# VectorE's operations with two SBUF operands given PSUM operands, and the five mixed streams finished by VectorE

## The reference

```python
# layer 0, per batch
x = x + attention(layernorm(x) -> q, k, v; 16 heads of 16, one mask for all batches) @ w_ao + b_ao
x = x + attention(layernorm(x) -> q; encoder -> k, v; mask per batch) @ w_co + b_co
#   scores = q.k / 4 * mask - 10000 * (1 - mask), softmax over the keys
x = x + gelu(layernorm(x) @ w1 + b1) @ w2 + b2
# layer 1, per batch (32 heads of 8)
xn = layernorm(x); sx = shift(xn) - xn
m  = tanh((xn + sx * maa_x) @ maa_w1) @ maa_w2            # five streams
x5 = xn + sx * (maa_stack + m)                            # w, k, v, r, g
w  = exp(-exp(td + tanh(x5[1] @ decay_w1) @ decay_w2))
r, k, v, g = x5[3] @ Wr.T, x5[0] @ Wk.T, x5[2] @ Wv.T, silu(x5[4] @ Wg.T)
# over the tokens: out = r.(u * k v + s); s = k v + w * s
x = x + (groupnorm over 8(out) * gn_w + gn_b) * g @ Wo.T
xn = layernorm(x); sx = shift(xn) - xn                    # then a gated squared-relu layer
x = x + sigmoid((xn + sx * fmr) @ Wr2.T) * (square(relu((xn + sx * fmk) @ Wk2.T)) @ Wv2.T)
```

## Time and profile before

| | |
|---|---|
| time, median of 3 runs | 743.11 us (741.23 to 743.57) |
| the profiled execution's own time | 742.92 us |
| its span, first to last instruction | 741.1 us |
| PE busy | 646.6 us (87% of the span) |
| DVE busy | 592.4 us (80%) |
| ACT busy | 574.4 us (78%) |
| POOL busy | 368.8 us (50%) |
| mean granted TensorE clock | 0.945 of full speed |

### The profile page before, as it was taken

How to read it: one execution, slowest core, us unless ns; L and a number is a source line. 1 busy time by engine, 2 the same in 40 slices (tenths; PEclk the granted TensorE clock), 3 DMA queues, 4 the chain that set the end, 5 groups by cost and what they waited for, 6 DMA issues and landing times. The chain is left out here.

```text
span 741.1 us, 16759 instructions
## 1 busy us (share of the span) xinstructions
PE 646.6 (87%) x5585; PEld 542.6 (73%) x5585; DVE 592.4 (80%) x1434; ACT 574.4 (78%) x2002; POOL 368.8 (50%) x537
## 2 busy tenths in 40 slices
...
GB/s 302 319 34 8 2 69 62 62 68 52 86 18 120 2 136 2 136 1 138 1 124 13 94 44 79 59 65 74 31 106 2 136 1 128 2 128 5 123 8 7
DMA packets 54844, 52.76 MB, mean 71 GB/s; under 512 B 6127, under 2 KB 49511, under 8 KB 54375
## 3 DMA queue, kind: packets, MB, share of 16 engines
...
## 5 line engine op out<-in xcount | busy, mean ns | idle before, releaser
L1067 ACT ACTIVATE SC<-SC,NMX 128x128 f32<-128x128 f32 x512 | 198.8, 394 | 6.8 <-DVE NMX L822 6.5
L1067 ACT ACTIVATION_READ_ACCUMULATOR SC<-SC,NMX 128x1 f32 x512 | 99.1, 194 | 0.0
L557 PE MATMUL PS_T<-CST,SC 128*128 128x128 f32 x512 | 81.3, 283 | 15.8 <-ACT SC L1067 6.4
L822 DVE TENSOR_REDUCE NMX<-SC 128x4 f32<-128x512 f32 x128 | 85.0, 668 | 3.4 <-POOL SC L1239 3.1
L799 DVE TENSOR_TENSOR SC<-PS_S,MASK 128x512 f32<-128x512 f32 x128 | 82.8, 670 | 5.9 <-PE PS_S L539 5.9
L1075 ACT ACTIVATE PT<-PS_T 128x512 f32<-128x512 f32 x128 | 77.0, 601 | 11.2 <-PE PS_T L557 10.2
L557 PEld LDWEIGHTS PS_T<-CST,SC 128*128 128x128 f32 x512 | 59.2, 144 | 30.6 <-ACT SC L1067 16.2
L894 DVE TENSOR_TENSOR_SCAN SS<-W,AJ 128x1024 f32<-128x1024 f32 x32 | 73.2, 2286 | 2.5 <-DVE AJ L887 0.5
L469 PE MATMUL PS_B<-B_LT,W 128*128 128x128 f32 x512 | 67.7, 290 | 7.5 <-ACT B_LT L1023 7.4
L469 PEld LDWEIGHTS PS_B<-B_LT,W 128*128 128x128 f32 x512 | 63.6, 203 | 11.4 <-ACT B_LT L1023 11.0
L1289 POOL TENSOR_TENSOR SS<-SS,KR 128x1024 f32<-128x1024 f32 x16 | 37.8, 2364 | 55.9 <-DVE SS L894 55.9
...
## 6 DMA issues: line engine op xcount, KB each, us to landing
...
```

The costliest lines, as they stand in the source:

```text
L557: last = pe.transpose(PS_T[:, j * T:(j + 1) * T], SC[:, nr(b, a) % 2, g, j, :], ident)
L822: dve.tensor_reduce(NMX[:, nr(b, a) % 2, GH * g:GH * g + GH], SC[:, nr(b, a) % 2, g], AX_X, ALU.max, negate=True)\
L1067: last = act.activation(SC[:, nr(b, a) % 2, g, j, :], SC[:, nr(b, a) % 2, g, j, :], ACT.Exp, bias=NMX[:, nr(b, a) % 2, h:h + 1], accum_out ...
```

## The change

- The three masks of `DVE_ADDS` are multiplied in place in PSUM, and their add reads PSUM and writes `SC`. The wait for the free half of `SC` moves from the multiplication to the add. TensorE's next writers of those banks wait for the add (`scores_read`).
- `b_streams` works in place in PSUM. `b_addnorm` goes to VectorE: three operations (128 x 512, 128 x 512, 128 x 256) from PSUM and `XN` into `MX`. The fifth stream's `b_low2`, `b_decay1` and `b_keyrec` wait for the first, second and third of them.
- `d_ruk` becomes one operation without u, which goes into a selector `USEL` made once; VectorE's `d_own` becomes one operation instead of two; `d_norm` goes from GpSimd to VectorE.
- The small tiles `GM`, `GV` and `GY` of the group norm move from SBUF to the last columns of `PS_D`; ScalarE's `d_affine` writes `PS_D` instead of SBUF, and `d_gated` reads it there.
- Five small steps of GpSimd (the mask's 10000*(mask-1), the copies of the previous rows, of the first columns and of the first states) go to ScalarE; the one-time scaling of `fv` moves into `d_shift`.
- All five order lists are new. They begin at another point of the round, so lags in them aren't those of the lists before.

```diff
 SP_ORDER = [
+    ("d_store", 0, 6), ("b_wspread", 0, 3), ("a_load", 0, 0), ("b_vstore", 0, 3), ("b_vspread", 0, 3)]
 PE_ORDER = [
+    ("b_low2", 0, 4), ("a_prob_turn", (1, 1), 3), ("d_own", 0, 5), ("a_scores", 0, 1), ("a_prob_turn", (1, 2), 3),
+    ("b_low2", 2, 4), ("d_read", 0, 5), ("a_prob_turn", (1, 3), 3), ("b_decay1", 0, 4), ("d_oturn", 0, 5),
+    ("b_decay2", 0, 4), ("a_pv", 1, 3), ("a_enc_turn", 0, 2), ("b_keyrec", 0, 4), ("b_keyrec", 1, 4),
+    ("a_out", 1, 3), ("a_turn", 1, 2), ("b_valgate", 0, 4), ("b_valgate", 1, 4), ("a_val", 1, 2), ("a_key", 1, 2),
+    ("a_prob_turn", (0, 0), 1), ("a_query", 1, 2), ("d_yturn", 0, 5), ("a_prob_turn", (0, 1), 1), ("a_scores", 1, 2),
+    ("d_out", 0, 5), ("b_turn", 0, 3), ("a_prob_turn", (0, 2), 1), ("b_mlp1", 0, 3), ("a_turn", 0, 0),
+    ("b_mlp1", 1, 3), ("b_mlp2", 0, 3), ("d_turn", 0, 5), ("a_prob_turn", (0, 3), 1), ("b_mlp2", 1, 3),
+    ("a_query", 0, 0), ("a_pv", 0, 1), ("d_keyrec", 0, 5), ("b_turn", 1, 3), ("a_val", 0, 0), ("d_keyrec", 1, 5),
+    ("a_key", 0, 0), ("a_out", 0, 1), ("b_low1", 0, 3), ("d_val", 0, 5), ("a_prob_turn", (1, 0), 2)]
 DVE_ORDER = [
+    ("a_normal", 0, 1), ("d_sum", 0, 6), ("a_mask", (1, 1), 3), ("a_mask", (1, 2), 3), ("a_maxima", (1, 0), 3),
+    ("d_stats", 0, 6), ("a_mask", (1, 3), 3), ("d_moments", 0, 6), ("a_addmask", (1, 3), 3), ("d_ruk", 0, 5),
+    ("a_inverse", 0, 2), ("a_maxima", (1, 1), 3), ("d_normal", 0, 6), ("d_outer", 0, 5), ("d_scan", 0, 5),
+    ("b_sum", 0, 4), ("b_stats", 1, 4), ("d_mixed", 0, 6), ("b_moments", 1, 4), ("a_query", 0, 1),
+    ("a_maxima", (1, 2), 3), ("b_normal", 1, 4), ("d_mixed", 1, 6), ("d_outer", 1, 5), ("a_maxima", (1, 3), 3),
+    ("a_context", 0, 2), ("b_mixed", 0, 4), ("d_rstate", 0, 5), ("a_sum", 0, 2), ("d_scan", 1, 5),
+    ("d_mixing", 0, 6), ("a_stats", 1, 2), ("b_streams", 0, 4), ("a_moments", 1, 2), ("b_addnorm", 0, 4),
+    ("d_own", 0, 5), ("b_streams", 1, 4), ("b_addnorm", 1, 4), ("b_streams", 2, 4), ("a_mask", (0, 0), 1),
+    ("a_inverse", 1, 3), ("a_mask", (0, 1), 1), ("d_output", 0, 5), ("a_addmask", (0, 1), 1), ("b_addnorm", 2, 4),
+    ("d_means", 0, 5), ("d_centre", 0, 5), ("a_maxima", (0, 0), 1), ("a_context", 1, 3), ("d_spread", 0, 5),
+    ("a_normal", 1, 2), ("a_maxima", (0, 1), 1), ("d_guess", 0, 5), ("d_guess", 1, 5), ("a_mask", (0, 2), 1),
+    ("a_mask", (0, 3), 1), ("d_guess", 2, 5), ("d_newton", (0, 0), 5), ("a_stats", 0, 0), ("d_newton", (0, 1), 5),
+    ("a_moments", 0, 0), ("d_newton", (0, 2), 5), ("a_sum", 1, 3), ("d_newton", (1, 0), 5), ("b_stats", 0, 3),
+    ("d_newton", (1, 1), 5), ("d_newton", (1, 2), 5), ("a_addmask", (0, 3), 1), ("d_newton", (2, 0), 5),
+    ("d_newton", (2, 1), 5), ("b_moments", 0, 3), ("d_newton", (2, 2), 5), ("d_norm", 0, 5), ("a_maxima", (0, 2), 1),
+    ("a_query", 1, 2), ("a_maxima", (0, 3), 1), ("d_gated", 0, 5), ("b_normal", 0, 3), ("b_gate", 0, 4),
+    ("a_mask", (1, 0), 2)]
 ACT_ORDER = [
+    ("b_scale", 0, 3), ("a_exps", (0, 3, 0), 1), ("a_exps", (0, 3, 1), 1), ("b_gelu", 0, 3),
+    ("a_prob_copy", (0, 2), 1), ("b_gelu", 1, 3), ("a_scale", 0, 0), ("d_scale", 0, 5), ("a_prob_copy", (0, 3), 1),
+    ("a_exps", (1, 0, 0), 2), ("a_widen", 0, 1), ("a_exps", (1, 0, 1), 2), ("a_exps", (1, 1, 0), 2),
+    ("a_spread", 0, 1), ("b_scale", 1, 3), ("a_exps", (1, 1, 1), 2), ("d_keyrec", 0, 5), ("a_val", 0, 0),
+    ("d_relu2", 0, 5), ("a_exps", (1, 2, 0), 2), ("a_exps", (1, 2, 1), 2), ("b_low", 0, 3), ("a_key", (0, 0), 0),
+    ("a_prob_copy", (1, 0), 2), ("a_key", (0, 1), 0), ("a_exps", (1, 3, 0), 2), ("a_prob_copy", (1, 1), 2),
+    ("d_own", 0, 4), ("a_exps", (1, 3, 1), 2), ("a_prob_copy", (1, 2), 2), ("d_ocopy", 0, 4),
+    ("d_first_states", 0, 3), ("b_decay1", 0, 3), ("a_prob_copy", (1, 3), 2), ("a_widen", 1, 2), ("b_decay2", 0, 3),
+    ("b_decays", 0, 3), ("a_lessmask", 0, 1), ("a_spread", 1, 2), ("d_squares", 0, 4), ("a_enc_copy", 0, 1),
+    ("a_exps", (0, 0, 0), 0), ("b_keyrec", 0, 3), ("a_exps", (0, 0, 1), 0), ("a_scale", 1, 1),
+    ("a_exps", (0, 1, 0), 0), ("b_values", 0, 3), ("a_exps", (0, 1, 1), 0), ("a_val", 1, 1), ("b_gatetanh", 0, 3),
+    ("a_key", (1, 0), 1), ("a_prob_copy", (0, 0), 0), ("a_key", (1, 1), 1), ("d_affine", 0, 4),
+    ("a_exps", (0, 2, 0), 0), ("a_exps", (0, 2, 1), 0), ("a_prob_copy", (0, 1), 0)]
 POOL_ORDER = [
+    ("a_addmask", (0, 2), 1), ("a_addbias", 0, 1), ("b_root", 0, 3), ("d_final", 0, 6), ("a_root", 0, 0),
+    ("b_addbias", 0, 3), ("a_addmask", (1, 0), 2), ("a_addmask", (1, 1), 2), ("a_addmask", (1, 2), 2),
+    ("d_root", 0, 5), ("d_shift", 0, 5), ("b_root", 1, 3), ("b_shift", 0, 3), ("d_rstate", 0, 4),
+    ("a_addmask", (0, 0), 0), ("a_root", 1, 1), ("a_addbias", 1, 2)]
...
+        USEL = sb("USEL", [CT, P // RS])
...
+        GM, GV, GY = (PS_D[:, 512 - n * RH:512 - (n - 1) * RH] for n in (1, 2, 3))
...
+        def scores_read(pe, n, g):
+            if n >= 0:
+                b, a = turn_of(n)
+                if (a, g) in DVE_ADDS:
+                    pe.wait_ge(a_dadded, nth(DVE_ADDS, b, (a, g)))
+                else:
+                    pe.wait_ge(a_masked, 4 * n + g + 1)
...
             def a_query(b, a):
-                pe.wait_ge(a_masked, 4 * nr(b, a))
+                scores_read(pe, nr(b, a) - 1, 3)
...
             def b_low2(b, n):
-                    pe.wait_ge(b_mix, 3 * b + 1)
+                    pe.wait_ge(b_mx, 3 * b + 1)
...
             def b_decay1(b, _):
-                pe.wait_ge(b_mx, 3 * b + 1)
-                pe.wait_ge(b_mix, 3 * b + 2)
+                pe.wait_ge(b_mx, 3 * b + 2)
...
-                    pe.wait_ge(b_mx, 3 * b + 2)
-                    pe.wait_ge(b_mix, 3 * b + 3)
+                    pe.wait_ge(b_mx, 3 * b + 3)
...
-                    last = pe.matmul(PS_D[:, t * (P // RS):(t + 1) * (P // RS)], RK[:, t, :], hsel,
+                    last = pe.matmul(PS_D[:, t * (P // RS):(t + 1) * (P // RS)], RK[:, t, :], USEL[:, t, :],
...
-                dve.tensor_tensor(SC[:, nr(b, a) % 2, g], PS_S[:, g], over_heads(mask), ALU.mult).then_inc(a_masked, 1)
+                masked = PS_S[:, g] if arg in DVE_ADDS else SC[:, nr(b, a) % 2, g]
+                dve.tensor_tensor(masked, PS_S[:, g], over_heads(mask), ALU.mult).then_inc(a_masked, 1)
...
-                dve.tensor_tensor(SC[:, nr(b, a) % 2, g], SC[:, nr(b, a) % 2, g], over_heads(MADD[:, b % 2 if a else 2, :]), ALU.add)\
+                if nr(b, a) > 1:
+                    dve.wait_ge(a_turned, 4 * nr(b, a) + g - 7)
+                dve.tensor_tensor(SC[:, nr(b, a) % 2, g], PS_S[:, g], over_heads(MADD[:, b % 2 if a else 2, :]), ALU.add)\
...
-                        last = dve.scalar_tensor_tensor(MX[:, i, t, :], PS_B[:, n % 2, at:at + T], col("stack", 2 * i + t),
-                                                        SX[:, t, :], ALU.add, ALU.mult)
+                        last = dve.scalar_tensor_tensor(PS_B[:, n % 2, at:at + T], PS_B[:, n % 2, at:at + T],
+                                                        col("stack", 2 * i + t), SX[:, t, :], ALU.add, ALU.mult)
...
+            def b_addnorm(b, n):
+                dve.wait_ge(b_mix, 3 * b + n + 1)
+                i, k = MIX_TURNS[n][0], len(MIX_TURNS[n])
+                dve.tensor_tensor(MX[:, i:i + 3 * k - 2:3], PS_B[:, n % 2, 0:k * C].rearrange("p (k t n) -> p k t n", t=CT, n=T),
+                                  XN[:, :, 1:T + 1].unsqueeze(1).to_broadcast([P, k, CT, T]), ALU.add).then_inc(b_mx, 1)
...
+                dve.tensor_tensor(RK[:, :, :], KR[:, 1], KR[:, 0], ALU.mult).then_inc(d_rk, 1)
...
+                dve.tensor_tensor(heads(CV[:, :]), heads(PS_D[:, C:2 * C]), over_tokens(OW[:, :], RH, RS), ALU.mult)\
+                    .then_inc(d_cv, 1)
...
+            def d_norm(b, _):
+                dve.wait_ge(d_gr, 12 * b + 12)
+                dve.tensor_tensor(heads(O[:, :]), heads(O[:, :]), over_tokens(GY[:, :], RH, RS), ALU.mult)\
+                    .then_inc(d_n, 1)
...
-                dve.scalar_tensor_tensor(YT[:, :, :], YA[:, :, :], 0.5, tiles(G[:, :]), ALU.mult, ALU.mult)\
+                dve.scalar_tensor_tensor(YT[:, :, :], tiles(PS_D[:, C:2 * C]), 0.5, tiles(G[:, :]), ALU.mult, ALU.mult)\
...
+                act.activation(PREV[:, b, :, :], tiles(values)[:, :, 0:2], ACT.Copy).then_inc(a_prev, 1)
...
+                act.activation(MADD[:, b % 2, :], MASK[:, b, :], ACT.Copy, bias=-10000.0, scale=10000.0)\
+                    .then_inc(a_less, 1)
...
+                    act.activation(XN[:, :, 0:1], PREV[:, b, :, 1:2], ACT.Copy)
...
+                act.activation(AJ[:, :, :, 0:1], S0[:, b, :, :].unsqueeze(3), ACT.Copy).then_inc(d_s0, 1)
...
+                    last = act.activation(PS_D[:, C + t * T:C + (t + 1) * T], PS_D[:, t * T:(t + 1) * T], ACT.Identity,
...
+                act.activation(XM[:, :, 0:1], PREV[:, b, :, 0:1], ACT.Copy)
```

(13 more changed lines are left out.)

135 lines of the change are left out of this document (32 added, 103 removed).

## The result

The changed kernel takes 735.15 us (median of 5 runs, 734.43 to 736.32), the kernel before 741.84 beside it on the same chip: ratio 0.9909, 95% interval 0.9886 to 0.9933. It is faster by 0.9%, 6.7 us. The profiled execution took 736.32 us, its span is 734.5; before, 742.92 and 741.1.

What follows compares the result with a forecast made beforehand. It saw three nearly full engines, with hand-overs between VectorE, GpSimd and TensorE setting the 39.24 us period. A period of 38.8 gave -5.3 us, the drain +0.4, so 742.92 became 738; own range 734 to 741, 80% range 729 to 751.

Steps and rivals of the forecast that it cites:

- The knot: Hand-overs VectorE, GpSimd, VectorE, TensorE around b_normal set the period; its 0.95 us VectorE wait and 0.46 for YT go.
- the fill: The start of the run before the repeating periods: priced at 0, from -1 to +1 us.
- Part (1): VectorE from the first b_addnorm to the end of d_norm: 13.45 us, every operand from elsewhere in time.
- part (3): Four streams, moments, b_addnorm and hand-overs at the end of the round: 1.8 us.
- Part (2): TensorE from d_yturn to the end of the next b_low2: 23.3 us, down from 25.3.
- The allowance of 0.3 for ScalarE: Added to the walked period of 38.5 us, giving 38.8, because ScalarE would be 94% full in strict list order.
- The drain: End of the run: decay matrix chain +1.0 us, d_norm -0.3 for each of the last two batches; net +0.4.
- PSUM writes: VectorE's surcharge for writing PSUM: taken as 0, bounded by -45 and +45 ns per operation, -1.4 to +1.4 us per period.
- rival (c): Slower: VectorE becomes the bound from streams to d_norm, gain gone at 14 ns on 32 operations; 749 to 755 us, 24%.
- GpSimd relief priced at nothing: GpSimd loses some 5 us of 23.20 per batch, worth nothing since it hides behind the three other engines.
- Rival (a): The knot is cut and nothing else binds: TensorE's idle time nearly all goes, -1.1 us per period, 729 us; 8%.
- Rival (b): ScalarE's added 0.8 us takes back the gain: period 39.0 to 39.3, time 741 to 744 us; 18%.

Runs made afterwards that it cites:

- e4: Changed kernel, but in the first round only TensorE makes values and keys ahead of the queries: 731.47 us, ratio 0.9852 to the kernel before.
- e10: Changed kernel with only the mixed streams back in SBUF: 742.59 us, ratio 1.001 to the kernel before.
- e12: Changed kernel plus five unused 128 x 512 adds per batch on GpSimd: 780.01 us, ratio 1.0505 to the kernel before.
- e1: Changed kernel with its new lists, but every operand moved to PSUM back in SBUF: 763.49 us, ratio 1.0294 to the kernel before.
- e2: Changed kernel with all moved operands back in SBUF and b_addnorm and d_norm back on GpSimd: 769.9 us, ratio 1.0371 to the kernel before.
- e3: Changed kernel's operations in the order lists of the kernel before, moved pieces at their nearest places: 811.5 us, ratio 1.092 to the kernel before.
- e8: Changed operations in the old order lists, with VectorE's masked scores going through SC again: 757.9 us, ratio 1.0232 to the kernel before.

## Why the prediction was right, and where it was not

The forecast was 738 us with its own range from 734 to 741; 735.15 lies in it, and the likeliest case held. The knot was read rightly, but that the total came so near is in part luck: the period gained twice what was forecast, and the fill lost what was priced at nothing. Step by step:

The knot. Right: b_normal no longer waits for GpSimd, d_out no longer for YT, and the scores have no visible wait for QT, where 0.3 was forecast. Nor had they one of 0.23 before: of the 0.23 us that the two waits leave of TensorE's 1.15, the profile has 0.07 in front of the scores (383.46 + 0.60 to 384.13 in the earlier trace rows) and 0.15 in front of a transpose of the cross attention's output, at 412.94. "The wait for B_LT stays": the latency of 1.31 us did, its price fell from 0.46 to 0.32.

The walk of the round. Part (1), whose nine operations of 512 columns leave out the first add (part (3) has it), was forecast at 13.45 and is 13.47, from the end of that add at 370.41 to 383.88. Part (3), from the streams at 406.95 to the end of the add at 408.79, is 1.84 against 1.8; 0.17 more is the hand-over from d_norm to TensorE. Part (2), forecast 23.3, runs between the same two points as 383.24 and 408.53 did, 384.05 to 406.95, and is 22.90: the term was mis-sized by 0.4. Of that, 0.14 is the wait for B_LT, which shrank, and 0.04 the gap in front of the scores; the rest lies in the durations taken off and was not followed up. The walk alone gave 38.5 and the measured period is 38.39.

The allowance of 0.3 for ScalarE is the step that failed most: nothing in the trace needed it. ScalarE at 35.96 of 38.39 holds up TensorE for 0.32 in one place, where it did before. An engine's list that was not walked was given a price instead of being read. Gain per period 0.87 instead of 0.44, eleven times: 4.7 us.

The fill, "priced at 0, from -1 to +1": wrong, +5.2 us between the two profiled executions, and this hid the error above in the total. How much of it is the lower granted clock and how much the order isn't shown. The first round of a new order has to be walked like any other: e4, with one exchange in it, is 3.7 us faster (ratios 0.9852 and 0.9909, whose intervals lie apart).

The drain. The decay matrix started 4.75 us behind its streams (669.25 to 674.00) against 2.81, +1.9 where +1.0 was forecast. From the last gate to the V8-fed d_outer it was 8.56 against 8.35, so only 0.2 came through. d_norm's move gave what was forecast, 0.42 against 0.63. Net +0.14 against +0.4.

PSUM writes, priced 0 within 45 ns: 350 against 339 for the streams, and e10, with these lists and the output in SBUF, has 340. The masks take 684 against 670, but in the changed kernel those that write SC take 684 as well, so this isn't the place of the output. The Newton steps are at 178 to 191 ns against 188 to 189. So the ten streams pay 10 ns each and the rest nothing that can be told apart; rival (c), which decides at 14 ns on 32 operations, did not come about. The mask adds: 686, priced at 670, against 711 before.

"GpSimd relief priced at nothing" was wrong in its reason, by e12 and e1. What the operands in PSUM buy is freedom from the other engine: in the old lists the Newton steps took 188 ns each with both inputs in SBUF, in the new ones the three of L981 with both inputs in SBUF take 304 on the mean (e1), since one of them stands beside a GpSimd operation and takes 660. The forecast compared operand places only by their read time, which is equal, and never asked what runs beside them; had it counted this, an SBUF version of these lists would have been forecast slower, as it is.

The kernel before had a hold of this kind too, and the forecast has no term for it: a_normal, a tensor_scalar of 128 x 256 with one tensor input, in SBUF. By line before and after, and one of its executions before with GpSimd's beside it:

```profile
L767 DVE TENSOR_SCALAR A_N<-X,A_MV,A_RS 128x256 f32<-128x256 f32 x32 | 17.9, 558 | 2.0 <-POOL A_RS L1197 1.8
...
L781 DVE TENSOR_SCALAR A_N<-X,A_MV,A_RS 128x256 f32<-128x256 f32 x32 | 13.0, 406 | 1.3 <-POOL A_RS L1237 1.3
```

```profile
387.45 0.69 DVE L767 TENSOR_SCALAR A_N<-X,A_MV,A_RS 128x256 f32<-128x256 f32 x1
...
387.27 0.72 POOL L1210 TENSOR_TENSOR X<-X,ROW 128x256 f32<-128x256 f32 x1
```

It ends at 388.14, 0.15 after GpSimd's operation. At two per batch the change gives VectorE back 0.30 us per period here, and the busy time of 37.26 came near the forecast 37.2 with its help. It is the order that does it: with b_addnorm on GpSimd again in the new lists (e2) a_normal takes 417 ns, in the old lists 742 (e3) and 809 (e8).

Rival (a), the knot cut and nothing else, comes nearer than its 8% said: of its 1.1 us per period 0.87 came. In the total it was hidden by the fill. Rival (b) did not happen.
